# The last expert layer in units of two sizes: 256 and 128 rows

## The reference

```
N = B * C;  E, K, I = 8, 2, 256;  cap = int(N * K * 1.25 / E)    # N = 4096, cap = 1280
logits = x @ Wg.T
top_v, top_i = top_k(logits, K);  gates = softmax(top_v)
pos = position of (token, choice) among the earlier rows of the same expert
keep = pos < cap
h = expert_batches @ W1[e]              # width 128 -> 512: "inp" and "gate"
h = gelu(inp) * gate                    # 256 wide
y = h @ W2[e]                           # back to width 128
out[token] = sum over its two choices of gate * y[its row]   (0 where not kept)
x = x + out
```

## Time and profile before

| | us |
|---|---|
| median of three runs | 1468.93 |
| lowest and highest run | 1465.43, 1472.74 |
| span of the profiled execution | 1467.0 |
| TensorE / VectorE / ScalarE / GpSimd busy in it | 1171.7 / 988.9 / 667.1 / 538.9 |
| units of the last layer: first transpose to last copy of a result | 1280.9 to 1435.9 |

### The profile page before, as it was taken

How to read it: one execution, slowest core, us unless ns; L and a number is a source line. 1 busy time by engine, 2 the same in 40 slices (tenths; PEclk the granted TensorE clock), 3 DMA queues, 4 the chain that set the end, 5 groups by cost and what they waited for, 6 DMA issues and landing times. The chain is left out here.

```text
span 1467.0 us, 34935 instructions
## 1 busy us (share of the span) xinstructions
PE 1171.7 (80%) x11141; PEld 918.1 (63%) x11154; DVE 988.9 (67%) x2920; ACT 667.1 (45%) x1423; POOL 538.9 (37%) x590
## 2 busy tenths in 40 slices
PE   2699994439999957779987879999799956499991
PEld 1477773338899925556673456677477755399991
DVE  3689996474443347998984679888477777766552
ACT  1367762105555503345564546766234343144440
POOL 2324201664235256534411232431121125752554
PEclk9999997559999967899998989999799988599996
DMA  6887743012223258435532177564200042133542
GB/s 179 206 215 191 188 124 129 29 33 87 77 92 109 75 133 209 122 101 144 150 84 51 44 176 167 150 163 106 86 1 0 0 152 74 53 120 106 149 140 73
DMA packets 138978, 164.58 MB, mean 112 GB/s; under 512 B 15308, under 2 KB 118754, under 8 KB 131728
## 3 DMA queue, kind: packets, MB, share of 16 engines
q1 hardware_dynamic: 130664, 146.62, 37.0%
q0 software_dynamic: 8192, 16.46, 4.1%
HBM read 111.98 MB, written 51.38 MB: 111 GB/s over the span
## 5 line engine op out<-in xcount | busy, mean ns | idle before, releaser
L586 DVE TENSOR_REDUCE A_neg_max<-A_s_bank 128x4 f32<-128x512 f32 x384 | 253.2, 688 | 46.3 <-PE A_s_bank L725 35.9
L448 ACT ACTIVATE A_probsT<-A_st_bank 128x512 f32<-128x512 f32 x384 | 222.4, 602 | 40.4 <-PE A_st_bank L738 39.2
L725 PE MATMUL A_s_bank<-A_k_stack,A_q_stack 72*128 72x128 bf16 x1536 | 157.5, 228 | 38.0 <-DVE A_neg_max L586 22.3
L738 PE MATMUL A_st_bank<-A_q_stack,A_k_stack 128*128 128x128 bf16 x1536 | 153.1, 224 | 7.1 <-DVE A_q_stack L602 6.2
L738 PEld LDWEIGHTS A_st_bank<-A_q_stack,A_k_stack 128*128 128x128 bf16 x1536 | 112.5, 103 | 52.2 <-issue 42.9
L725 PEld LDWEIGHTS A_s_bank<-A_k_stack,A_q_stack 72*128 72x128 bf16 x1536 | 106.3, 102 | 52.1 <-DVE A_neg_max L586 33.4
L752 PE MATMUL A_pv_bank<-A_probsT,A_v_pad 128*32 128x128 f32 x3072 | 127.4, 284 | 1.5 <-issue 1.5
L2041 ACT ACTIVATE E_h<-E_h_bank,w_L_b 128x256 f32<-128x256 f32 x184 | 76.8, 471 | 72.4 <-PE E_h_bank L2141 71.0
L2153 PE MATMUL E_y_bank<-E_w,E_h 128*128 x736 | 90.3, 276 | 2.2 <-ACT E_h L2041 0.9
L752 PEld LDWEIGHTS A_pv_bank<-A_probsT,A_v_pad 128*32 128x32 f32 x3072 | 74.1, 111 | 24.7 <-issue 3.4
L2141 PE MATMUL E_h_bank<-E_xT,E_w_u 128*128 128x256 f32 x368 | 88.8, 386 | 0.0
(11 more groups left out here) (371 smaller groups left out, 2641.4 us busy)
## 6 DMA issues: line engine op xcount, KB each, us to landing
A_q_stack<-q_scratch SPq DMA_DIRECT2D x48, 576.0 KB
A_k_stack<-k_scratch SPq DMA_DIRECT2D x32, 576.0 KB
q_scratch<-A_q_parts SPq DMA_DIRECT2D x48, 192.0 KB, 2.3
A_k_stack<-k_scratch SPq DMA_DIRECT2D x48, 192.0 KB
E_xe<-slots_in SPq DMA_DIRECT2D x53, 128.0 KB, 2.1
slots_out<-E_ye SPq DMA_DIRECT2D x53, 128.0 KB, 1.7
A_ctxT<-in_ctxT SPq DMA_DIRECT2D x24, 256.0 KB, 10.5
k_scratch<-A_k_parts SPq DMA_DIRECT2D x32, 192.0 KB
```

The costliest lines, as they stand in the source:

```text
L448: act.activation(probsT[n % 2][:, c * HQ:(c + 1) * HQ, :], st_bank[c % 2][:, :].rearrange("k (a q) -> k a q", a=HQ), ACT.Exp, scale=scale) ...
L586: dve.tensor_reduce(neg_max[:, c * HQ:(c + 1) * HQ], s_bank[c % 2][:, :].rearrange("q (a k) -> q a k", a=HQ), AX.X, ALU.max, negate=True). ...
L725: last = pe.matmul(s_bank[c % 2][:, a * S:(a + 1) * S], q_stack[slot][0:COMBO, h, at:at + S], k_stack[slot][0:COMBO, h, at:at + S], start= ...
L738: last = pe.matmul(dst, k_stack[slot][:, h, at:at + S], q_stack[slot][:, h, at:at + S], start=True, stop=spread)
```

## The change

A part now has n / 256 units of 256 rows and eight units of 128 rows (`ST = 128`), one for each expert, in place of the seven more of 256. That makes 16 + 8, 8 + 8 and 8 + 8, in all 56 units, 32 of 256 rows and 24 of 128. Unit u no longer has column u of the tables: the lists `column` and `rows_of`, made when the program is built, interleave the sizes. Part 0 runs 256, 256, 128, 256, 256, 128, ...; parts 1 and 2 run 256, 128, 256, 128, ... A 128-row unit has one transpose, eight matmuls of 128 columns, four result matmuls, and half of the columns in each ScalarE and VectorE operation on its data; `copy_w1` is the same for both sizes.

`table` works out both sizes. The terms of a part move out of its third piece into a new function, `pieces_of_experts`, of 22 operations, since five terms in place of three now map a token to its result row; `out_rows` works on five. The pieces of `table(1)` come at u = 4, 5, 6 and those of `table(2)` at u = 12, 13, 14; `pieces_of_experts` at u = 3, 11, 19; `out_rows` at u = 14, 16, 20, 22. The additions begin at u = 28 and u = 52, one for each 3/2 units. Before the first unit, `table(0)` runs in one go, as before.

```diff
-    UT = 256
-    unit_counts = [2 * (last - first) * CT // UT + NE - 1 for first, last in PARTS]
+    UT, ST = 256, 128
+    wholes = [2 * (last - first) * CT // UT for first, last in PARTS]
+    unit_counts = [n + NE for n in wholes]
     first_units = [sum(unit_counts[:p]) for p in range(len(PARTS) + 1)]
     NU = max(unit_counts)
     last_unit = first_units[-1]
-    MOST = CT * max(last - first for first, last in PARTS) // UT
-    ADDS = {0: 26, 1: 45}
+    MOST = CT * max(last - first for first, last in PARTS) // ST
+    column, rows_of = [], []
+    for p, n in enumerate(wholes):
+        for e in range(NE):
+            for i in (*range(e * n // NE, (e + 1) * n // NE), n + e):
+                column.append(first_units[p] + i)
+                rows_of.append(UT if i < n else ST)
+    ADDS = {0: 28, 1: 52}
+
+    def out_row(u):
+
+        p = part_of_unit[u]
+        i = column[u] - first_units[p]
+        return min(i, wholes[p]) * UT + max(i - wholes[p], 0) * ST
...
-            return min(ADDS[p] + (b - PARTS[p][0] * RT) * 5 // 4, last_unit) if p in ADDS else last_unit
+            return min(ADDS[p] + (b - PARTS[p][0] * RT) * 3 // 2, last_unit) if p in ADDS else last_unit
...
+                w, n, at = wholes[p], unit_counts[p], first_units[p]
+                kinds = ((slice(0, w), w, cut[:, 1:]), (slice(w, n), NE, left[:, 1:]))
+                per_u = lambda v, n: v[:, None, :].to_broadcast([S, n, NE])
+                per_e = lambda v, n: v[:, :, None].to_broadcast([S, n, NE])
+                numbers = core.iota_units
...
-                    own.did(dve.tensor_scalar(lim[:, :], held[:, :], -float(UT), 0.0, ALU.add, ALU.max))
+                    for i, size in enumerate((UT, ST)):
+                        own.did(dve.tensor_scalar(lims[:, i, :], held[:, :], -float(size), 0.0, ALU.add, ALU.max))
                     own.link(dve.tensor_tensor(square[:, :, :], held[:, :, None].to_broadcast([S, NE, MOST]),
                                                steps[:, None, :].to_broadcast([S, NE, MOST]), ALU.is_gt))
-                    own.link(dve.tensor_reduce(units[:, :], square[:, :, :], AX.X, ALU.add))
-                    own.link(dve.tensor_tensor(square[:, :, 0:NE], upto[:, :, :],
-                                               units[:, None, :].to_broadcast([S, NE, NE]), ALU.mult))
-                    own.link(dve.tensor_reduce(ends[:, :], square[:, :, 0:NE], AX.X, ALU.add))
+                    own.did(dve.tensor_reduce(counts[:, 0, :], square[:, :, :], AX.X, ALU.add))
+                    own.link(dve.tensor_reduce(counts[:, 1, :], square[:, :, 1::2], AX.X, ALU.add))
+                    own.link(dve.tensor_tensor(sums[:, :, :, :], upto[:, None, :, :].to_broadcast([S, 2, NE, NE]),
+                                               counts[:, :, None, :].to_broadcast([S, 2, NE, NE]), ALU.mult))
+                    own.link(dve.tensor_reduce(ends[:, :, :], sums[:, :, :, :], AX.X, ALU.add))
+                    own.link(dve.tensor_scalar(cut[:, 1:], ends[:, 1, :], float(w), None, ALU.min))
+                    own.did(dve.tensor_tensor(taken[:, :], cut[:, 1:], cut[:, 0:NE], ALU.subtract))
+                    own.link(dve.scalar_tensor_tensor(left[:, 1:], cut[:, 1:], -2.0, ends[:, 0, :], ALU.mult, ALU.add))
                 if 1 in pieces:
-                    own.link(dve.tensor_tensor(hit, per_u(ends[:, :]), per_e(numbers), ALU.is_le))
+                    for of, many, until in kinds:
+                        own.did(dve.tensor_tensor(hit[:, of, :], per_u(until, many), per_e(numbers[:, 0:many], many), ALU.is_le))
+                    own.wait()
                     own.link(dve.tensor_reduce(which[:, 0:n], hit[:, :, 0:NE - 1], AX.X, ALU.add))
-                    own.link(dve.tensor_tensor(hit, hit, per_u(ends[:, :]), ALU.mult))
+                    for of, many, until in kinds:
+                        own.did(dve.tensor_tensor(hit[:, of, :], hit[:, of, :], per_u(until, many), ALU.mult))
+                    own.wait()
                     own.link(dve.tensor_reduce(begun[:, 0:n], hit[:, :, 0:NE - 1], AX.X, ALU.max))
                     own.did(dve.tensor_copy(expert_of[:, at:at + n], which[:, 0:n]))
-                    own.did(dve.tensor_tensor(begun[:, 0:n], numbers, begun[:, 0:n], ALU.subtract))
+                    for of, many, _ in kinds:
+                        own.did(dve.tensor_tensor(begun[:, of], numbers[:, 0:many], begun[:, of], ALU.subtract))
...
+                    own.link(dve.tensor_tensor(hit, per_u(core.iota8[:, :], n), per_e(which[:, 0:n], n), ALU.is_equal))
+                    own.link(dve.tensor_tensor(taken_hit[:, :, :], hit[:, w:n, :], per_u(taken[:, :], NE), ALU.mult))
+                    own.did(dve.tensor_reduce(skipped[:, :], taken_hit[:, :, :], AX.X, ALU.add))
+                    for i, (of, many, _) in enumerate(kinds):
+                        own.did(dve.tensor_tensor(hit[:, of, :], hit[:, of, :], per_u(lims[:, i, :], many), ALU.mult))
+                    own.wait()
+                    own.did(dve.tensor_reduce(row[:, 0:n], hit, AX.X, ALU.add))
                     own.did(dve.tensor_scalar(which[:, 0:n], which[:, 0:n], float((last - first) * CT),
                                               float(first * NE * CT), ALU.mult, ALU.add))
-                    own.link(dve.scalar_tensor_tensor(row[:, 0:n], begun[:, 0:n], float(UT), row[:, 0:n], ALU.mult, ALU.min))
+                    own.link(dve.scalar_tensor_tensor(begun[:, w:n], skipped[:, :], 2.0, begun[:, w:n], ALU.mult, ALU.add))
+                    for (of, _, _), size in zip(kinds, (UT, ST)):
+                        own.did(dve.scalar_tensor_tensor(row[:, of], begun[:, of], float(size), row[:, of], ALU.mult, ALU.min))
+                    own.wait()
                     own.link(dve.tensor_tensor(row[:, 0:n], row[:, 0:n], which[:, 0:n], ALU.add))
                     own.link(dve.tensor_copy(row_of[:, at:at + n], row[:, 0:n]))
-                    own.did(dve.scalar_tensor_tensor(terms[:, p, 2, :], units[:, :], float(UT), lim[:, :], ALU.mult, ALU.subtract))
-                    own.did(dve.tensor_tensor(terms[:, p, 1, :], lim[:, :], begins[:, p, :], ALU.add))
-                    own.link(dve.tensor_tensor(terms[:, p, 0, :], ends[:, :], units[:, :], ALU.subtract))
-                    own.did(dve.tensor_scalar(terms[:, p, 2, :], terms[:, p, 2, :], -float(UT), None, ALU.add))
-                    own.link(dve.scalar_tensor_tensor(terms[:, p, 0, :], terms[:, p, 0, :], float(UT), begins[:, p, :],
-                                                      ALU.mult, ALU.subtract))
                     dve.sem_inc(table_done, 1)
+
+            def pieces_of_experts(p):
+
+                begin, threshold, step, second, second_step = (terms[:, p, i, :] for i in range(5))
+                after, far = float(wholes[p] * UT), 4.0 * TOK
+                own.did(dve.tensor_tensor(many[:, :], left[:, 1:], left[:, 0:NE], ALU.subtract))
+                own.did(dve.scalar_tensor_tensor(threshold, taken[:, :], float(UT), lims[:, 1, :], ALU.mult, ALU.min))
+                own.did(dve.tensor_scalar(step, left[:, 0:NE], float(ST), after, ALU.mult, ALU.add))
+                own.did(dve.scalar_tensor_tensor(other[:, :], cut[:, 1:], float(UT), lims[:, 0, :], ALU.mult, ALU.subtract))
+                own.did(dve.scalar_tensor_tensor(second_step, left[:, 1:], float(ST), lims[:, 1, :], ALU.mult, ALU.subtract))
+                own.link(dve.scalar_tensor_tensor(begin, cut[:, 0:NE], float(UT), begins[:, p, :], ALU.mult, ALU.subtract))
+                own.did(dve.tensor_scalar(many[:, :], many[:, :], 0.0, None, ALU.is_gt))
+                own.did(dve.tensor_tensor(threshold, threshold, lims[:, 0, :], ALU.subtract))
+                own.did(dve.scalar_tensor_tensor(step, taken[:, :], -float(UT), step, ALU.mult, ALU.add))
+                own.did(dve.tensor_scalar(other[:, :], other[:, :], -float(UT), None, ALU.add))
...
+                own.link(dve.scalar_tensor_tensor(step, cut[:, 0:NE], -float(UT), step, ALU.mult, ALU.add))
 
...
-                                              pick[:, k:k + 1, chunk(c), :].to_broadcast([S, 3, RT, NE]),
-                                              terms[:, p, :, None, :].to_broadcast([S, 3, RT, NE]), ALU.mult))
+                                              pick[:, k:k + 1, chunk(c), :].to_broadcast([S, 5, RT, NE]),
+                                              terms[:, p, :, None, :].to_broadcast([S, 5, RT, NE]), ALU.mult))
                 own.wait()
                 own.link(dve.tensor_reduce(chosen[:, :, :, :].rearrange("t c k b -> t c (k b)"), weighed[:, :, :, :],
                                            AX.X, ALU.add))
                 own.did(dve.tensor_tensor(chosen[:, 0, :, :], chosen[:, 0, :, :], slot[:, :, chunk(c)], ALU.add))
-                own.link(dve.tensor_tensor(chosen[:, 1, :, :], slot[:, :, chunk(c)], chosen[:, 1, :, :], ALU.is_ge))
```

(30 more changed lines are left out.)

87 lines of the change are left out of this document (52 added, 35 removed).

## The result

The changed kernel takes **1482.94 us** (1479.48 to 1486.18, 5 runs) beside 1468.93 before (5 runs): ratio 1.0073, 95% interval 1.005 to 1.0096. This ratio, as recorded, stands for 10.7 us; the two medians by themselves are 14.0 apart (1.0095). In the four later sets of runs the kernel before had medians of 1471.5 to 1473.2, which speaks for the smaller figure. So the changed kernel is slower, by 11 to 14 us. I had forecast 1473 with a range of 1461 to 1479, and the change inside what a measurement can tell: wrong, on the slow side.

A forecast was written before the change was run, and what follows sets the result against it. TensorE's queue was taken to bound the kernel, VectorE and GpSimd close behind. Part 0 ending 9.2 us later uses up GpSimd's 6.44 idle: +3.1, with 0.9 allowed, 1468.9 + 4 = 1473 us, range 1461 to 1479.

The forecast's parts named there:

- the first cluster: Part 0, u = 3 to 6: VectorE's work 16.1 us against TensorE's 9.4; less 1.7 slack, 5.0 us of stall.
- the rule: VectorE's small operations on n columns: 0.20 + (n - 8)/960 us linked, 0.08 + (n - 8)/960 unlinked.
- Rivals 1 and 2: Less VectorE lag in part 0, earlier gathers: 1454.5 us, 16%; all of TensorE's saving counts: 1444 us, 3%.
- can only add; I allow 0.9: Allowance for TensorE's clock and denser small rows beside the paced gathers: 0.9 us on the forecast.
- a rival of 20%, at +5: TensorE's clock falls in part 0's stalls, pushing part 0 back another 4 to 8 us: 1478 us, 20%.
- the stalls of all three clusters count: Reading of the skill: each idle gap in part 0's three clusters throttles TensorE anew, giving the clock rival's time, 1478 us.
- 0 of the 0 to 0.8 that I had bounded: TensorE's register load in each short unit, taken as 0 us because `hidden` (0.89) exceeds the load's 0.84.
- the change's -25 us: Saving by TensorE's time alone over parts 0, 1 and 2, a 128-row unit costing 1.44 us against 2.84.
- not 9.2: Part 0's end: 17.5 us of TensorE stalls less 8.3 saved, so 9.2 us later.
- the saving was to be -8.3: TensorE's work in part 0 falls from 65.3 to 57.0 us, saving 8.3.
- not 77.7: GpSimd's gathers of parts 0 and 1 need 77.4 us, then 0.3 before part 2's, the 6.44 idle gone.
- the forecast's +3.1: GpSimd's gathers of part 2 begin at 1441.4 in place of 1438.3, 3.1 us later: span 1470.1.

The follow-up runs named there:

- e1: Changed kernel with VectorE's extra work spread, so no two adjacent units carry it, some of it moved out of part 0: 1470.8 us, ratio to before 0.9991.
- e9: Changed kernel with VectorE reading the expert's number right behind its gate product, ahead of the unit's extra work: 1476.66 us, ratio to before 1.0023.
- e5: Changed kernel with unused float32 matmuls, 0.7 to 4.0 us, on TensorE ahead of seven results that had waited: 1478.85 us, ratio to before 1.0045.
- e14: e11 with a fixed expert's second weights in the 128-row units, so TensorE reads no number there: 1455.69 us, ratio to before 0.9907.
- e11: e1 plus VectorE's early read of the expert's number, without the pacing wait in GpSimd's gathers: 1460.45 us, ratio to before 0.9911.
- e6: e1 with TensorE's transpose for unit u + 2 placed ahead of `hidden` of unit u + 1: 1474.63 us, ratio to before 1.0022.
- e7: e4 with TensorE's transpose for unit u + 2 placed ahead of `hidden` of unit u + 1: 1474.21 us, ratio to before 1.0007.
- e3: Kernel before, without the pacing wait in GpSimd's gathers of parts 0 and 1: 1469.47 us, ratio to before 0.9992.
- e4: e1 without the pacing wait in GpSimd's gathers of parts 0 and 1: 1471.01 us, ratio to before 0.998.
- e8: Kernel before, without short units, with its extra work at the units where the change puts it: 1478.5 us, ratio to before 1.0042.
- e12: e8 with ten unused float32 products (2.2 us) on TensorE ahead of the result of u = 15: 1476.25 us, ratio to before 1.0021.

## Why the prediction was wrong, step by step

- **The direction of the shift was right.** TensorE's saving did not reach the end; VectorE stalled it in part 0, and GpSimd's gathers of parts 0 and 1 went through without idle and set the end. The stalls of the first cluster came at u = 4 to 7 (0.75, 1.13, 0.89, 2.09 us; forecast 5.0, measured 4.9), then 2.10, 0.23 and 4.64 at u = 13 to 15 (forecast 9.0, measured 7.0), then 3.2 from u = 20 on, 2.34 of it at u = 21 (forecast 4.1). The pieces read above cost what the rule gave (`out_rows` 3.1, the third piece of a table 2.4); e1 and e9 show the mechanism and the bare read. Rivals 1 and 2 fell.
- **The failed step: the clock, in the sum's "can only add; I allow 0.9".** The clock is a term of 4.4 us in part 0 (e5). In that pair of executions it is 5.5 at the end, of which 1.1 is the gathers' own (78.6 us in place of 79.7). I had it as a rival of 20%, at +5: about the size, but outside the sum. The earlier trace rows showed a fall behind one gap, and the longest stall of the forecast, near 5 us, was longer than that gap (3.2 us ahead of the result that it held up), so the likeliest case should have held the term. The section that I named, "HAM oscillation — how this bites in real kernels" of "TensorE: Matmul & The Clock Gate" in the Trainium skill, says that the array is throttled again behind idle gaps that last long enough and pays for its warm-up each time; my "the stalls of all three clusters count" took it too widely. The traces agree in part: falls followed the waits of 2.09 (u = 7) and 4.64 (u = 15), and none followed those of 2.10 (u = 13) and 2.34 (u = 21).
- **The second term put at nothing: the short unit, 1.6 to 1.9 us, not 1.44.** I took 0 of the 0 to 0.8 that I had bounded, with the reason that `hidden` covers the read. e14 bears that reason out, and yet the unit costs 0.2 to 0.5 more (1.94 at the place read in e1; a pair takes 4.46 in e11's tightest stretches, where 4.28 was forecast; nearly 0.4 on average in e1 and in e11). The results of such a pair on e11's TensorE:

```profile
1359.24 1.06 PE L2865 MATMUL E_y_bank<-E_w,E_h 128*128 x8
...
1361.97 0.61 PE L2865 MATMUL E_y_bank<-E_w,E_h 128*128 x4
...
1363.70 1.06 PE L2865 MATMUL E_y_bank<-E_w,E_h 128*128 x8
```

  At the place read in e1, 0.21 of it is the wait for ScalarE's copy of x; what the remainder is stays open, since e6 and e7 missed their aim. It is why the change's -25 us was never to be had: in e11 the last result comes 11.9 us earlier than before, 4.0 of the missing 13.2 are waits for VectorE's product, and 9 are the short units.
- **Part 0 ends 15.4 us later, not 9.2.** On TensorE's own timeline of the kernel after, the waits for VectorE's product are 15.0 us (forecast 17.5) and half-speed work behind them costs 4.3 (forecast 0). What is left of the 15.4 is -3.9 where the saving was to be -8.3. So 4.4 were lost besides: some 0.5 in a longer stretch at the lower clock with which the stage begins (a clock of 0.61 in its first 8 us, where before has 0.68), the rest about 0.5 for each of eight short units. The two terms at nothing were in part offset, by luck, by waits 2.5 us shorter than forecast. These are shares of one timeline: a short unit that costs more inside a cluster shortens the wait behind it. Only the clock's part was measured by taking it away (4.4 of the 6.2); the other 1.8 is what is left.
- **The gathers took 79.7 us to part 2's first, not 77.7.** Against before's 83.8, with its idle time, this is -4.1 in place of -6.1, 2 us more. No run tests the cause; the same paced gathers took 78.6 in e5 and 77.3 in e9.
- **The sum.** The stage is +15.4 - 4.1 = +11.3 longer, beside the forecast's +3.1: 4.4 by the clock, 1.8 by part 0's rest, 2.0 by the gathers. The recorded ratio, 1.0073, is 10.7 us; of the 14.0 between the two medians, 2.7 would lie outside the stage.

## What to carry to other kernels

When the busiest engine gets less to do, add up the next engine's work unit by unit, with its waits and register reads, where the extra work stands; halving a unit halves the time in which a neighbour may be late. A long stall of TensorE can have a second price in the clock behind it: over all runs here, 10 of TensorE's 17 waits for VectorE's product of 1.86 us or more went with a fall, and a fall cost some 1.5 to 2.6 us (an estimate from the clock and the work done at it, and from e8 beside e12). Put it into the likeliest case, not into a rival alone, once the forecast itself contains such stalls. A limit that isn't the bound (pacing, e3 and e4) measures as free, and becomes worth some 5 to 6 us when the others are gone (e11): try it again after each step.

## What I had not expected of the hardware

- A read of a register from SBUF on VectorE, with its wait for the table, costs 0.78 to 0.9 us bare behind a chain that it waited for, and shows as a gap of 0.24 in e9 (VectorE at 1329.60), where it is issued behind an independent product of 0.4 us, with a chain after it. At the place compared above e9 saved 0.65 us.
- A wait of TensorE of 1.86 us was followed by a fall of its clock (e6, rows above), one of 2.86 in the same run was not. e8's 2.46 us went with a fall (0.85 in the 4 us with the stall, 0.73 in the next 4), at 1.5 us; filled with unused products the clock stayed at 1.00 (e12). So the length of the wait alone doesn't decide, and what does is not shown here.
- One float32 product of 128 columns shows as two instructions of 0.11 us.
